# Turning the first chunk's gated heads on VectorE instead of TensorE, and moving its output projection behind the last feed-forward tile

## What is computed

```python
xn = _layernorm(x, axis=-1)
x = x + mlstm(xn) + ffn(xn)
# mlstm: q, k, v, gates from xn; a recurrent state over the tokens gives h
h_norm = multihead_norm(h, gamma)          # 8 heads of 64
h_out = sigmoid(o_preact) * h_norm
y = h_out @ Wout.T                         # 512 -> 512
# ffn: hidden 2048
gated = silu(xn @ w_gate.T) * (xn @ w_up.T)
out = gated @ w_down.T
```

## Time and profile before

| What | Value |
|---|---|
| Median of 3 runs | 3110.75 us (3110.28 to 3111.6) |
| Profiled execution, its own time | 3110.59 us |
| Its span | 3108.9 us |
| TensorE busy | 3047.3 us, 98% of the span |
| VectorE busy | 2347.1 us, 75% |
| ScalarE busy | 1113.4 us, 36% |
| GpSimd busy | 781.7 us, 25% |
| Mean granted TensorE clock | 0.998 of 2.4 GHz |

### The profile page before, as it was taken

One profiled execution on the slowest core, in us unless ns is written; L12 is line 12 of the kernel. 1 busy time (PEld: TensorE's weight loads), 2 busy tenths in 40 slices (PEclk: granted clock), 3 DMA queues, 4 the chain that ended last, 5 costly groups with the idle time before them and its releaser, 6 DMA issues.

```text
span 3108.9 us, 62468 instructions
## 1 busy us (share of the span) xinstructions
PE 3047.3 (98%) x22090; PEld 2194.9 (71%) x22090; DVE 2347.1 (75%) x5913; ACT 1113.4 (36%) x2160; POOL 781.7 (25%) x1121
## 2 busy tenths in 40 slices
PE   4999999999999999999999999999999999999999
PEld 2677777777777777777777777777777777777776
DVE  7877777777777777777777777777777777777777
ACT  6333333333323333333333333333233333333332
POOL 4222222222222222222222222222222222222222
PEclk9999999999999999999999999999999999999999
DMA  5000000000000000000000000000000000000000
GB/s 224 8 14 13 13 7 7 13 13 13 13 0 13 13 13 13 7 7 13 13 13 13 7 7 13 13 13 13 0 13 13 13 13 7 7 13 13 13 13 7
DMA packets 20334, 51.09 MB, mean 16 GB/s; under 512 B 1506, under 2 KB 1634, under 8 KB 18274
## 3 DMA queue, kind: packets, MB, share of 16 engines
q1 hardware_dynamic: 20322, 50.95, 4.4%
HBM read 34.16 MB, written 16.78 MB: 16 GB/s over the span
## 4 chain that ended last, share of the span: by engine, by line
issue 73%; POOL 22%; PE 2%; DVE 1%; POOLq 1%; ACT 1%; DMA 0%; SPq 0%; DVEq 0%; ACTq 0%
POOL arena L555 9%; POOL pair_r L545 4%; POOL small L574 3%; POOL arena L565 2%; POOL begun L562 1%; POOL small L462 1%; DVE amax L757 1%; PE work L1154 0%; POOLq L554 0%; DMA arena<-w_v_dram 0%; POOL small L464 0%; POOL small L467 0%; POOL small L460 0%; PE work L1119 0%; ACT weights L611 0%
## 5 line engine op out<-in xcount | busy, mean ns | idle before, releaser
L1117 PE MATMUL work<-xt,weights 128*128 128x256 f16 x4608 | 1256.0, 273 | 0.0
L1119 PE MATMUL work<-xt,weights 128*128 128x256 f16 x4608 | 1256.0, 273 | 0.0
L1118 PE MATMUL work<-xt,weights 128*128 128x256 f16 x4608 | 1255.9, 273 | 0.0
L555 POOL TENSOR_TENSOR arena<-arena 128x256 f16<-128x256 f32 x512 | 359.5, 702 | 1628.2 <-ACT arena L689 1628.2
L689 ACT ACTIVATE arena<-arena 128x256 f16<-128x256 f32 x512 | 213.3, 417 | 1057.8 <-DVE arena L983 1057.8
L1117 PEld LDWEIGHTS work<-xt,weights 128*128 128x128 f16 x4608 | 478.5, 104 | 69.2
L1118 PEld LDWEIGHTS work<-xt,weights 128*128 128x128 f16 x4608 | 450.9, 98 | 69.7
L1119 PEld LDWEIGHTS work<-xt,weights 128*128 128x128 f16 x4608 | 450.8, 98 | 52.3
L1117 PE MATMUL acc<-weights,arena 128*128 128x512 f16 x1024 | 388.1, 379 | 0.5 <-POOL arena L555 0.5
L1118 PE MATMUL acc<-weights,arena 128*128 128x512 f16 x1024 | 388.1, 379 | 0.0
L1119 PE MATMUL acc<-weights,arena 128*128 128x512 f16 x1024 | 388.1, 379 | 0.0
(11 more groups left out here) (212 smaller groups left out, 4150.7 us busy)
## 6 DMA issues: line engine op xcount, KB each, us to landing
arena<-x_dram SPq DMA_DIRECT2D x33, 512.0 KB, 3.4
out_dram<-arena SPq DMA_DIRECT2D x32, 512.0 KB, 2.8
weights<-w_g_dram SPq DMA_DIRECT2D x4, 1024.0 KB, 13.2
weights<-w_u_dram SPq DMA_DIRECT2D x4, 1024.0 KB, 20.4
arena<-w_d_dram SPq DMA_DIRECT2D x4, 1024.0 KB, 27.2
arena<-w_qk_dram SPq DMA_DIRECT2D x1, 1024.0 KB, 6.3
arena<-w_v_dram SPq DMA_DIRECT2D x1, 1024.0 KB, 8.3
weights<-w_o_dram SPq DMA_DIRECT2D x1, 1024.0 KB, 25.4
```

What stands on the lines that cost most here:

```text
L555: g.tensor_tensor(hh[:, j % HB, 1, :], tt[:, j % 2, :], hh[:, j % HB, 0, :], ALU.subtract).then_inc(h_ready, 1)
L1117: t.matmul(dst, w[0], a[0], start=first, stop=False, skip_group_check=True)
L1118: t.matmul(dst, w[0], a[1], start=False, stop=False, skip_group_check=True)
L1119: return t.matmul(dst, w[1], a[0], start=False, stop=last, skip_group_check=True)
```

## The change

The transposes of chunk 0's gated heads leave TensorE. VectorE makes them, as it makes those of x, in four quarters of four transposes, the steps `hturn00` to `hturn03` behind tiles 11, 13 (two) and 14, into an SBUF place `hot`; ScalarE and VectorE split from there (`hoT0`, now behind tile 14). The projection `att0` moves behind tile 15, and stands behind `hoT1` there. `hof` and the split buffer get a place of their own for each chunk. `hoT0` leaves the rotation of the banks: it has 32 uses in place of 33, and each use from tile 12 on sits in another bank. `att0` takes bank 0 and `att1` bank 1, which the next block's gates and q need. In the diff below, the first `hoT` part is ScalarE's, the second and `hturn` are VectorE's, and the last is TensorE's.

```diff
-         "ffn6", "st0", "ffn7", "ffn8", "st1", "ffn9", "ffn10", "st2", "ffn11", "hoT0", "ffn12", "st3", "o1",
-         "ffn13", "att0", "ffn14", "ffn15", "hoT1", "att1"])
+         "ffn6", "st0", "ffn7", "ffn8", "st1", "ffn9", "ffn10", "st2", "ffn11", "ffn12", "st3", "o1",
+         "ffn13", "ffn14", "ffn15", "hoT1", "att0", "att1"])
...
+BANK["att0"], BANK["att1"] = 0, 1
...
-AFTER[11] = ["hoT0", "turn12", "turn13"]
+AFTER[11] = ["turn12", "turn13", "hturn00"]
 AFTER[12] = ["pv3", "o1", "center1"]
-AFTER[13] = ["att0", "scale1"]
-AFTER[14] = ["heads1"]
-AFTER[15] = ["hoT1", "xT0", "xT1"]
+AFTER[13] = ["scale1", "hturn01", "hturn02"]
+AFTER[14] = ["hturn03", "hoT0", "heads1"]
+AFTER[15] = ["hoT1", "xT0", "xT1", "att0"]
...
-                 ("hof", 512), ("hoh", 512), ("kp", 512), ("tt", 512), ("hh", 768), ("res", 1024),
+                 ("hof", 512), ("hof2", 512), ("hoh", 1024), ("kp", 512), ("tt", 512), ("hh", 768), ("res", 1024),
...
+        hot = arena[:, starts["bc"]:starts["bc"] + D]
...
                         elif step.startswith("hoT"):
-                            wait_full(act, i, step)
-                            s.activation(ho[:, 0, :, :], bank(step)[:, :].rearrange("p (k t) -> p k t", k=KC),
-                                         ACT.Copy).then_inc(ho_hi, 1)
+                            if k == 0:
+                                act.wait_ge(heads_turned, START + (i + 1) * TURNS)
+                            else:
+                                wait_full(act, i, step)
+                            s.activation(ho[:, k, 0, :, :], (hot if k == 0 else bank(step)[:, :]).rearrange(
+                                "p (k t) -> p k t", k=KC), ACT.Copy).then_inc(ho_hi, 1)
...
                         elif step.startswith("hoT"):
                             dve.wait_ge(ho_hi, i * NCH + k_ + 1)
-                            d.tensor_tensor(ho[:, 1, :, :], bank(step)[:, :].rearrange("p (k t) -> p k t", k=KC),
-                                            ho[:, 0, :, :], ALU.subtract).then_inc(free_of(step), 1)
+                            ins = d.tensor_tensor(ho[:, k_, 1, :, :],
+                                                  (hot if k_ == 0 else bank(step)[:, :]).rearrange(
+                                                      "p (k t) -> p k t", k=KC),
+                                                  ho[:, k_, 0, :, :], ALU.subtract)
+                            ins.then_inc(ho_split if k_ == 0 else free_of(step), 1)
...
+                        elif step.startswith("hturn"):
+
+                            dve.wait_ge(ho_ready, START + i * NCH + 1)
+                            turn(hot, hof, k_, heads_turned)
...
                 def project(c):
 
-                    wait_drained(pe, i, f"hoT{c}")
+                    if c == 0:
+                        pe.wait_ge(ho_split, i + 1)
+                    else:
+                        wait_drained(pe, i, "hoT1")
...
-                        elif step.startswith("hoT"):
+                        elif step == "hoT1":
                             pe.wait_ge(ho_ready, START + i * NCH + k + 1)
```

More of the change, by code:

```diff
@@ L286, in mlstm_mlp_kernel @@
         num = at["num"].rearrange("p (h e) -> p h e", h=NH)
-        sq = at["hof"].rearrange("p (h e) -> p h e", h=NH)
+        sq = at["hof2"].rearrange("p (h e) -> p h e", h=NH)
         hof = at["hof"]
@@ L290, in mlstm_mlp_kernel @@
         kp = at["kp"].bitcast(F16).rearrange("p (a g t) -> p a g t", a=2, g=NG)
-        ho = at["hoh"].bitcast(F16).rearrange("p (a k t) -> p a k t", a=2, k=KC)
+        hot = arena[:, starts["bc"]:starts["bc"] + D]
+        ho = at["hoh"].bitcast(F16).rearrange("p (c a k t) -> p c a k t", c=NCH, a=2, k=KC)
         tt = at["tt"].rearrange("p (b t) -> p b t", b=2)
@@ L341, in mlstm_mlp_kernel @@
         xn_turned = sem("xn_turned")
+        heads_turned = sem("heads_turned")
+        ho_split = sem("ho_split")
         kt_ready = sem("kt_ready")
@@ L531, in _ @@
             for n, started in enumerate((*work_free, out_stored, res_done, exp_done, p_ready, num_ready, ho_ready,
-                                         state_ready, xn_turned)):
+                                         state_ready, xn_turned, heads_turned)):
                 g.memset(begun[0:1, n:n + 1], 0.0).then_inc(started, START)
@@ L817, in means, with turn @@
                     d.bn_aggr(mean_var[:, c, :], bn6[:, c, :]).then_inc(stats_ready, 1)
-            def turn(dst, src, q):
+            def turn(dst, src, q, done):
                 tokens = slice(q * 32, (q + 1) * 32)
@@ L824, in turn @@
                     d.transpose(dst.rearrange("p (k t) -> p k t", k=KC)[r * 32:(r + 1) * 32, :, tokens],
-                                features).then_inc(xn_turned, 1)
+                                features).then_inc(done, 1)
             def x_low(i, c, src):
@@ L1077, in _ @@
                             wait_drained(dve, i, f"o{k_}")
-                            d.scalar_tensor_tensor(out=hof.rearrange("p (h e) -> p h e", h=NH),
+                            d.scalar_tensor_tensor(out=(hof, at["hof2"])[k_].rearrange("p (h e) -> p h e", h=NH),
                                                    in0=to.rearrange("p (h e) -> p h e", h=NH), scalar=1.0,
@@ L1090, in _ @@
                             dve.wait_ge(xn_ready, NCH * (i + 1) + c + 1)
-                            turn(xnt[c], xn[c], k_)
+                            turn(xnt[c], xn[c], k_, xn_turned)
+                        elif step.startswith("hturn"):
+                            dve.wait_ge(ho_ready, START + i * NCH + 1)
+                            turn(hot, hof, k_, heads_turned)
                         elif step.startswith("kturn"):
@@ L1192, in project @@
                 def project(c):
-                    wait_drained(pe, i, f"hoT{c}")
+                    if c == 0:
+                        pe.wait_ge(ho_split, i + 1)
+                    else:
+                        wait_drained(pe, i, "hoT1")
                     for n in range(KC):
-                        mm_ = three(bank(f"att{c}")[:, :], (ho[:, 0, n, :], ho[:, 1, n, :]),
+                        mm_ = three(bank(f"att{c}")[:, :], (ho[:, c, 0, n, :], ho[:, c, 1, n, :]),
                                     (w_out[:, 0, n, :], w_out[:, 1, n, :]), n == 0, n == KC - 1)
@@ L1289, in _ @@
                                      stop=True).then_inc(work_full, 1)
-                        elif step.startswith("hoT"):
+                        elif step == "hoT1":
                             pe.wait_ge(ho_ready, START + i * NCH + k + 1)
                             for n in range(KC):
-                                tr = t.transpose(bank(step)[:, n * P:(n + 1) * P], hof[:, n * P:(n + 1) * P],
+                                tr = t.transpose(bank(step)[:, n * P:(n + 1) * P], at["hof2"][:, n * P:(n + 1) * P],
                                                  ident[:, :])
```

## The result

The changed kernel takes 3244.58 us (median of 4 runs, 3243.2 to 3245.58) against 3111.1 us of the kernel before in the same comparison. The ratio is 1.0429, 95% interval 1.0413 to 1.0444: the change makes the kernel 4.3% slower, 133 us. The forecast was 3231 with a range of 3190 to 3264.

The account below looks back on a forecast made before the run. TensorE, busy 98%, bounds the kernel, with VectorE's heads releasing `hoT1`. 3110.59 plus 32 x 2.79 for net waits and 31 x 0.24 for q gives 3207; clock dips add 24: 3231 us, range 3190 to 3264.

Parts of the forecast that it names:

- The gain: `hoT0` leaving TensorE before tile 12 saves 0.89 us a block: 0.43 wait and its start, 0.46 the four transposes.
- Tile 13's bank: TensorE waits at tile 13 for VectorE's L983 of tile 12 to free the bank, losing 0.5 us a block.
- The chain on VectorE: VectorE's steps from tile 13 through `heads1`, timed from like stretches, release TensorE for `hoT1` at about 1302.85.
- The pause at `hoT1`: TensorE arrives at `hoT1` at 1299.70 and waits 3.15 us a block for the heads of chunk 1.
- q: `att1` sits in the bank that q needs, so q waits 0.22 to 0.25 us on 31 blocks.
- A block without the clock: Each block grows by 2.79 us, plus 0.24 at q on 31 blocks: 3207 us in all.
- The clock: Pauses at `hoT1` halve TensorE's clock in 14 of 32 blocks, 1.7 us each: +24 us.
- Rival C: The clock falls behind the pause in every block: 3262 us, chance 0.12.
- B: The clock holds throughout: 3207 us (3195 to 3215), chance 0.2.
- E: Not slower: VectorE takes the sixteen transposes in its idle time before `hoT1`; 3090 us, chance 0.07.
- D: VectorE's chain overlaps more than its parts say, and the pause is 1.5 to 2 us: 3159 us, chance 0.09.
- The two rules that the prediction cites: Skill pages: gaps between matmul bursts drop the clock once each; 128x128 transposes go to TensorE wherever PSUM can take them.

Follow-up runs that it names:

- the kernel with the transposes later: Kernel before, with TensorE's `hoT0` moved from behind tile 11 to behind `o1` in tile 12: 3095.59 us against 3110.33, ratio 0.995.
- the filled pause: Changed kernel with 12 unneeded 512-column matmuls put ahead of TensorE's wait at `hoT1`: 3196.04 us.
- the load alone: Kernel before, with sixteen extra VectorE transposes of a spare buffer at the places of the change: 3187.26 us.
- the heads first: Changed kernel with VectorE's order behind tile 14 turned round, `heads1` ahead of `hturn03` and `hoT0`: 3241.53 us.

## Why the prediction was right, point by point

- **The gain, 0.89 a block.** Its wait, 0.43, is confirmed by the kernel with the transposes later (14.7 us, 0.46 a block). The other half, the transposes themselves, was not measured alone.
- **Tile 13's bank.** Forecast 0.50, measured 0.28. L980 of tile 12 was forecast at 1286.07 and came at 1286.05 (1336.05 less 50). What was too large is the allowance for the signal and the first weight load: 0.3, and the runs show 0.13 (L990 of tile 12 ends at 1336.92, tile 13 begins at 1337.05). This error only moves a part of the wait from `hoT1` to here.
- **The chain on VectorE.** Tile 7 and tile 9 were good patterns: the eight transposes were forecast at 1294.78 and began at 1294.65, tile 14 at 1297.45 against 1297.31, `hturn03` done at 1299.67 against 1299.53. The forecast is 0.13 too late throughout; this was there already at L980 of tile 13, put at 1292.24 and found at 1292.12. L1078 was given 0.85 and took 0.69. So TensorE was released at 1302.50 and not at 1302.85.
- **The pause at `hoT1`.** Forecast 3.15; from the last matmul of `down(13)` to the transposes it was 2.9, of which the profile counts 2.77 as idle.
- **q.** Forecast 0.24, measured 0.13. The wait begins when L927 (before L920) has drained the bank, as forecast; the signal was given 0.15 and took 0.06 (L927 runs from 1362.65 to 1363.40, and q begins at 1363.46).
- **A block without the clock.** Forecast +3.0, measured 97.1 - 94.5 = +2.6. The end of the wait at `hoT1` was put 0.35 too late and q 0.11 too long; the blocks give 0.4 for both together, 13 us in all.
- **The clock.** The size of a dip, 1.7 us, was right. The number of dips was the step that failed: 14 of 32 blocks, and it was 29. It rested on three pauses of the prologue, of which the one of 2.25 us left the clock alone. The runs show that a pause of 2.8 in the loop is enough nearly always. This error, 15 x 1.7 = 25 us, and the one of the waits, 13 us, have opposite signs, which is why 3231 lies as near to 3244.58 as it does; that much is luck. Rival C, with dips in every block, described the clock better than the forecast did.
- **The rivals.** B (the clock holds, 3207) is what the filled pause shows at 3196. E (not slower) is refuted by the load alone, 77 us slower. D did not come about.
- **The two rules that the prediction cites.** The warning of the Trainium skill, page "TensorE: Matmul & The Clock Gate", section "HAM oscillation — how this bites in real kernels", that the clock drops once for each gap, was nearer than my count: the trace has 29 dips for 32 pauses of 2.8 us. But the section words it for gaps longer than these; that pauses of 2.8 and even 1.9 us are enough, and that those of 1.33 and 1.5 bring no dip, is shown by the runs alone. The rule of the Trainium skill, page "VectorE: DVE Perf Modes", section "Rules for kernel authors", that sends 128x128 transposes to TensorE held: no version with VectorE's transposes came near to the kernel before, the best of them is 3147.62.

## What to carry to other kernels

Where an engine's share of idle time invites more work, follow its timeline to the next instruction that the bound engine waits for, and take the time of a like stretch of the same kernel for each added step. VectorE was busy 75% of the span and 70% of the 20 us that counted, and still had room for only 1.67 us there before TensorE would wait. When a bound TensorE gets a new pause, look at the granted clock too: the clock added more than half as much again to the pauses of 2.8 us, and nothing to those of 1.33 and 1.5. The wait for a late input was better removed here by moving the step one tile on than by taking the step away.

## What the runs showed that was not expected

Pauses that differ little cost very different amounts: mean clock 0.985 with 1.9 us of idle TensorE a block and 0.998 with 1.5 us, 44 us of run time apart. But the length of the pause is not all that decides. The pause is 2.76 to 2.78 us in all blocks of the changed kernel, and three of them have no dip. The first 1.5 us from the start of `hoT1`, in the first, fourth, seventh and eighth block behind one without a dip, and in the ninth, which is the next without one:

```profile
759.73:761.23 1.50, 1.50 (x6) 1.13 (x7) 0.70 (x2) 0.74 (x2) 0.24 (x1) 0.51 0.00 0
1056.12:1057.62 1.50, 1.50 (x7) 0.89 (x8) 0.70 (x2) 0.73 (x2) 0.24 (x1) 0.70 0.00 0
1352.50:1354.00 1.50, 1.50 (x8) 0.88 (x9) 0.70 (x2) 0.73 (x2) 0.24 (x1) 0.90 0.00 0
1451.31:1452.81 1.50, 1.50 (x9) 1.01 (x10) 0.70 (x2) 0.73 (x2) 0.24 (x1) 0.96 0.00 0
1550.10:1551.60 1.50, 1.50 (x9) 0.97 (x10) 0.70 (x2) 0.73 (x2) 0.24 (x1) 1.00 0.00 0
```

The third number from the end is the granted clock. The fall to half clock comes at once in the first of them (0.51) and 1.2 us behind the start in the seventh (0.90 is 0.3 us at half clock), so about 0.2 us later from each block to the next, until one is left out. The falls thus keep a distance of their own, 0.2 us more than that of the blocks, and are not tied to `hoT1`. So it matters also at what moment a pause falls. That would let the pause of 2.25 us in the prologue pass beside those of 1.9 in the loop, but no run moved a pause without changing its length, and this stays open.

The last step of the heads of chunk 1 took 1.04 us before, 0.69 in the changed kernel, and 1.04 again with the heads first. In the last case GpSimd's L560 runs into it (VectorE's and GpSimd's timelines, heads first):

```profile
1347.68 1.04 DVE L1086 SCALAR_TENSOR_TENSOR arena<-arena 128x512 f32<-128x512 f32 x1
```

```profile
1347.37 0.81 POOL L560 TENSOR_TENSOR arena<-arena 128x256 f16<-128x256 f32 x1 [2.38 <-ACT arena L694]
```

In the changed kernel GpSimd is idle at that time. All traces say the same: in the ten kernels this instruction runs 640 times, 224 times with GpSimd idle, and then it takes 0.69 to 0.70 us; the other 416 times GpSimd is at work beside it for 0.49 us or more, and it takes 0.95 to 1.04. The page "GPSIMD Engine Reference" of the Trainium skill, section "Specifications", says that it shares its SBUF interfaces with VectorE, with contention where VectorE's instruction has two SBUF inputs. This one has two, and the traces agree; the price here is 0.26 to 0.35 us. A chain that is moved in time changes such meetings, and with them its own length.
